# Attention and feed-forward on one core: transposes of the probabilities moved to the end of each TensorE step

## The reference

```python
q = jnp.einsum('btm,mhd->bthd', x, w_aq)
k = jnp.einsum('btm,mhd->bthd', x, w_ak)
v = jnp.einsum('btm,mhd->bthd', x, w_av)
q = _rope(q)
k = _rope(k)
s = jnp.einsum('bihd,bjhd->bhij', q, k) / D_HEAD
s = s - jnp.asarray(INF_APPROX, x.dtype) * mask
p = jax.nn.softmax(s, axis=-1)
o = jnp.einsum('bhij,bjhd->bihd', p, v)
r = jnp.einsum('bihd,hdm->bim', o, w_ao)
...
x = _layernorm(x + attention(x))
h = jax.nn.silu(_tlin(x, w1_w, w1_s)) * _tlin(x, w2_w, w2_s)
h = jax.nn.gelu(_tlin(h, h1_w, h1_s), approximate=False)
h = jax.nn.gelu(_tlin(h, h2_w, h2_s), approximate=False)
x = _layernorm(x + _tlin(h, w3_w, w3_s))
```

## Time and profile before

| | |
|---|---|
| median of 3 runs | 1065.4 us (1064.43 to 1065.68) |
| profiled execution, its own time | 1065.99 us |
| span of the profiled execution | 1064.2 us |
| PE busy | 997.1 us (94%) |
| DVE busy | 820.6 us (77%) |
| ACT busy | 593.3 us (56%) |
| POOL busy | 539.6 us (51%) |
| mean granted TensorE clock | 0.981 |

### The profile page before, as it was taken

How to read it: one execution, slowest core, us unless ns; L and a number is a source line. 1 busy time by engine, 2 the same in 40 slices (tenths; PEclk the granted TensorE clock), 3 DMA queues, 4 the chain that set the end, 5 groups by cost and what they waited for, 6 DMA issues and landing times. The chain is left out here.

```text
span 1064.2 us, 19686 instructions
## 1 busy us (share of the span) xinstructions
PE 997.1 (94%) x5648; PEld 860.2 (81%) x5648; DVE 820.6 (77%) x1803; ACT 593.3 (56%) x1255; POOL 539.6 (51%) x536
## 2 busy tenths in 40 slices
PE   3799999999999999999999999999839999999995
PEld 3688888898888889888888888888728878788784
DVE  5888888888888888887888888788555677486744
ACT  3566666665666666566666666666434252433521
POOL 4666767776676776677677666767250101000000
PEclk9899999999999999999999999999969999999998
DMA  8433233432322123323222222221020000000000
GB/s 282 150 127 74 61 80 97 124 99 56 75 69 69 49 59 100 70 61 79 59 49 59 61 70 68 72 59 40 1 80 1 1 1 21 1 20 0 1 20 21
DMA packets 33292, 66.16 MB, mean 62 GB/s; under 512 B 5457, under 2 KB 6993, under 8 KB 32209
## 3 DMA queue, kind: packets, MB, share of 16 engines
q1 hardware_dynamic: 30400, 58.62, 21.0%
q10 hardware_dynamic: 2832, 6.82, 1.7%
HBM read 24.26 MB, written 7.34 MB: 30 GB/s over the span
## 5 line engine op out<-in xcount | busy, mean ns | idle before, releaser
L703 POOL TENSOR_SCALAR probs<-probs,inv_sum 128x128 f32<-128x128 f32 (+7 forms) x256 | 191.1, 747 | 232.4 <-DVE inv_sum L621 231.8
L534 ACT ACTIVATE pT<-psum 128x512 fp32r<-128x512 f32 (+3 forms) x384 | 173.9, 490 | 144.0 <-PE psum L401 141.9
L308 PE MATMUL psum<-pT,vals 128*128 128x512 f32 (+3 forms) x1152 | 242.6, 351 | 1.6 <-DVE rT L663 1.6
L522 ACT ACTIVATE probs<-psum,neg_max 128x128 f32<-128x128 f32 (+7 forms) x256 | 190.5, 744 | 80.2 <-DVE neg_max L615 79.8
L615 DVE TENSOR_REDUCE neg_max<-psum 128x1 f32<-128x128 f32 (+7 forms) x256 | 191.2, 747 | 54.8 <-PE psum L392 53.6
L631 DVE TENSOR_TENSOR pT<-psum,pT 128x512 fp32r<-128x512 f32 (+3 forms) x384 | 200.7, 551 | 32.3 <-ACT pT L534 25.3
L308 PEld LDWEIGHTS psum<-pT,vals 128*128 128x128 f32 x1152 | 187.7, 189 | 23.9 <-DVE pT L631 1.7
L401 PE MATMUL psum<-ident,probs 128*128 128x128 f32 x1152 | 173.7, 277 | 12.9 <-POOL probs L703 12.2
L883 PE MATMUL ps<-hid,w 128*128 128x512 f32 x768 | 181.3, 396 | 0.0
L708 POOL TENSOR_TENSOR swapped<-by_cos,swapped 128x512 f32<-128x512 f32 x128 | 164.7, 1298 | 14.2 <-DMA swapped<-by_sin 14.2
L883 PEld LDWEIGHTS ps<-hid,w 128*128 128x128 f32 x768 | 143.7, 188 | 34.5
(11 more groups left out here) (77 smaller groups left out, 1195.3 us busy)
## 6 DMA issues: line engine op xcount, KB each, us to landing
swapped<-by_sin SPq DMA_DIRECT2D x256, 128.0 KB, 2.3
w_stage<-qk_split SPq DMA_DIRECT2D x30, 256.0 KB, 2.7
wv_stage<-v_split SPq DMA_DIRECT2D x15, 256.0 KB, 2.7
x_split<-ffn_raw ACTq DMA_DIRECT2D x2, 1024.0 KB, 5.8
ffn_raw<-g SPq DMA_DIRECT2D x2, 1024.0 KB, 8.0
x_moving<-x_split SPq DMA_DIRECT2D x2, 1024.0 KB, 5.1
out<-y SPq DMA_DIRECT2D x4, 512.0 KB, 2.6
raw_x<-xT SPq DMA_DIRECT2D x3, 512.0 KB, 11.6
```

The costliest lines, as they stand in the source:

```text
L308: ins = nc.tensor.matmul(out_ap, left[a], right[b], start=first and i == 0, stop=last and i == 2)
L522: nc.scalar.activation(probs[:, ib % 4, :width].rearrange("p (h c) -> p h c", h=halves), score_ps[:, ib % 2, :halves, :half], ACT.Exp, bia ...
L534: nc.scalar.activation(pT[chunk][:, 0, 4 * f:4 * f + n_blocks, (ib % 4) * P:(ib % 4 + 1) * P], bank("t", head[1], nth)[:, :n_blocks * P].r ...
L703: nc.gpsimd.tensor_scalar(p, p, inv_sum[:, n:n + 1], 1.0, ALU.mult, ALU.mult).then_inc(probs_ready[0], 1)
```

## The change

Within a step, PE now does the `qk` projections, the values and the pieces of the weighted sum right after the scores, and the transposes last. ACT takes the high part of the values ahead of that of the transposed probabilities, and DVE the rotation's products and the low part of the values ahead of the low part of the transposed probabilities. `plan_banks` follows the new order. POOL and SP are as they were.

```diff
@@ -77,9 +77,9 @@
-            after = ([("t", off, FIRST_FILL[s] + k) for k in range(FILLS_OF[s])]
-                     + [("qk", off + 1, j) for j in range(NQK) if QK_STEP[j] == s]
-                     + [("v", 0, c) for c in range(NV) if V_STEP[c] == NI * off + s])
+            after = ([("qk", off + 1, j) for j in range(NQK) if QK_STEP[j] == s]
+                     + [("v", 0, c) for c in range(NV) if V_STEP[c] == NI * off + s]
+                     + [("t", off, FIRST_FILL[s] + k) for k in range(FILLS_OF[s])])
@@ -463,8 +463,6 @@
                 if exists(ahead):
                     scores(ahead, (s + 2) % NI)
-                if exists(head):
-                    transpose_probs(head, s)
                 for target, j in rope_tasks(head, s, QK_STEP):
                     project_qk(step_on(target, -1), j)
                 for c in v_tasks(head, s):
@@ -473,6 +471,8 @@
                 if s in PV1_PIECES and exists(step_on(head, -1)):
                     attend(step_on(head, -1), 1, PV1_PIECES[s])
+                if exists(head):
+                    transpose_probs(head, s)
@@ -575,10 +575,10 @@
+                for c in v_tasks(head, s):
+                    values_high(head[0], c)
                 if exists(head):
                     transposed_high(head, s)
-                for c in v_tasks(head, s):
-                    values_high(head[0], c)
@@ -680,12 +680,12 @@
-                if exists(head):
-                    transposed_low(head, s)
                 for target, j in rope_tasks(head, s, QK_STEP):
                     rope_products(target, j)
                 for c in v_tasks(head, s):
                     values_low(head[0], c)
+                if exists(head):
+                    transposed_low(head, s)
```

## The result

The changed kernel took 1081.39 us (median of 4 runs, 1080.66 to 1082.54) against 1065.32 us before: a ratio of 1.0153, 95% interval 1.0136 to 1.0171. That is 16.1 us more; the profiled executions differ by 1080.66 - 1065.99 = 14.7 us. The forecast was 1086.5 us, with a range from 1073 to 1096.

What follows compares the result with a forecast made beforehand. PE was taken as the bound; 15 odd heads at +1.31 us (19.7), 15 even heads at +0.13 (2.0) and -0.7 at the end gave +21 us on 1065.99. Forecast 1086.5 us, range 1073 to 1096.

Steps and rivals of the forecast that it cites:

- What bounds, and what can be gained: PE bounds; odd heads' step 6 has stalls of 0.81 and 0.16 us, 0.97 us per odd head to gain.
- T to the scores of block 4, 5.62 us: Odd head, from its start (T, scores of block 2): bank 1 waits for DVE's low part of block 0, +0.72 us.
- Scores of block 4 to X, 7.62 us: Odd head, to the end of block 3's transposes (X): step 3's twelve matmuls come in ahead, +1.94 us on 5.68.
- X to the scores of block 0, 5.68 us: Block 3's transposes' end to next head's block 0 scores: POOL's low part of tile 1 sets it, -0.38 us.
- Odd head, +1.31 us: Each odd head's four stretches together: 0.72 + 1.94 - 0.38 - 0.97 us, paid by 15 odd heads.
- Even head, +0.13 us: Each of 15 even heads: 0.11 us of waiting for POOL's chain plus near misses in banks, 2.0 us in all.
- The attention's end, -0.7 us: Last head: of the 1.62 us wait for the addition into `rT`, 0.7 taken as gained; bounds 0 and 1.62.
- The sum: Whole kernel: 19.7 us from odd heads, 2.0 from even ones, -0.7 at the end, together +21 us.
- Only the POOL chain binds: Rival: DVE catches up in step 0, bank 1 costs nothing new, odd head pays 0.59 us; about 1076; chance 0.17.
- the clock swing in the attention: Rival: after each step 6 wait about 3 us run at 1.2 GHz, +45 us, about 1131; chance 0.03.
- more waits: Rival: waits for `rT` in step 1 and block 4's low part, 0.25 us in 30 heads; about 1094; chance 0.14.

Runs made afterwards that it cites:

- e9: The change with step 3 back in the old order and odd heads' banks remapped so block 0's transposes take bank 5, not 1: 1047.8 us.
- e10: The change in full, with the same bank map as e9: 1066.9 us.
- e1: The change with step 3 alone put back, its transposes ahead of the weighted sum's twelve matmuls: 1061.1 us.
- e4: The change with POOL's step 4 reordered, tile 1's low part ahead of block 5's multiplication and tile 2's rotation sum: 1068.1 us.
- e2: The change with step 7 alone put back, its transposes ahead of the weighted sum's six matmuls: 1079.5 us.
- e3: The change with steps 3 and 7 both put back in the order of before: 1061.8 us.
- e6: The kernel before, with bank 1 not lent in step 0 and nothing else: 1070.2 us.
- e5: The change with bank 1 not lent in step 0: 1084.6 us.
- e8: The kernel before with the new order in steps 6 and 7 only, and bank 1 not lent in step 0: 1083.1 us.
- e7: The change with step 3 in the order of before and bank 1 not lent in step 0: 1065.0 us.
- e11: The kernel before with the new order in steps 6 and 7 only, planner as it is (bank 1 lent in step 0): 1077.3 us.
- e12: The change with PE's order untouched, plus e10's bank map and e4's POOL order: 1054.3 us.

## Why the prediction was right, and where its terms were off

- **What bounds, and what can be gained.** Right. The stalls of step 6 in odd heads are gone, and from the scores of block 0 to the next head takes 452.79 - 448.30 = 4.49 us (forecast 4.56).
- **T to the scores of block 4, 5.62 us.** Measured 435.15 - 429.53 = 5.62 us. e9 and e10 show it as the meeting of DVE's lateness and one bank, worth 1.0 us in each odd head.
- **Scores of block 4 to X, 7.62 us.** Measured 442.70 - 435.15 = 7.55.
- **X to the scores of block 0, 5.68 us.** Measured 448.30 - 442.70 = 5.60, by the median 5.68. e1 and e4 break this chain at its two ends, TensorE's order and POOL's, and end 20.3 and 13.3 us under the change.
- **Odd head, +1.31 us.** By the medians +1.05 us. The four stretches changed by +0.72, +1.86, -0.41 and -1.13 us, where +0.72, +1.94, -0.38 and -0.97 were forecast: the waits are as forecast, and most of the difference is that groups of matmuls behind other neighbours cost a little less (below). That is 15 x 0.26 = 3.9 us less than forecast.
- **Even head, +0.13 us.** Wrong in sign: -0.19 us by the medians, a gain of 15 x 0.19 = 2.9 us where a loss of 2.0 us was forecast. X to the scores of block 0 came to 423.64 - 418.00 = 5.64 us, close to the forecast 5.68; what I had left out is the same effect of the neighbours. The stretch to X grew by 1.77 and not 1.94 us, since the twelve matmuls take 1.86 us behind the scores where they took 1.96 behind transposes, and the last stretch shrank by 0.15.
- **The attention's end, -0.7 us.** Wrong in sign: from the last head's T to the feed-forward part's first instruction it takes 788.59 - 758.60 = 29.99 us, 27.31 before: +2.7 us, outside the bounds that I had given. I had taken the wait for the addition into `rT` as partly gone. From the start of the last eight transposes to the group that waits for the addition it takes 3.35 us in the change and 3.36 before: the last piece of the weighted sum, 0.7 us, had stood in this stretch, now stands ahead of it and covers nothing, and the wait grew from 1.62 to 2.26 us. Two new waits at the last head's start (0.43 us for DVE's `pT`, 0.46 for `rT`) take the place of one of 0.45 us. These make 1.1 us; the other 1.6 us are TensorE's clock, below.
- **The sum** by these measured terms: 15 x 1.05 - 15 x 0.19 + 2.7, and 1.1 us less at the start (the first odd head's T is at 53.44, before at 54.51), is 14.5 us, against 14.7 between the profiled executions. The start may be chance: the other kernels have this T at 53.70 to 54.56.
- **The rivals.** "Only the POOL chain binds" did not happen, nor did the clock swing in the attention: 15 waits of about 1.0 us left it at full rate. Of "more waits", the bank that block 5's transposes need from block 4 is late in the change too, but this wait lies under the one for POOL and costs nothing; it shows when that one is lifted (e4).

The mechanism was right in both its parts. The forecast of 21 us against the profiles' 14.7 comes from the two terms wrong in sign and from the odd head's 0.26 us: 3.9 + 4.9 us too much, 3.4 us too little at the end, and 1.1 us not foreseen at the start; between the medians the change cost 16.1 us. That the total came within 5.1 us is in part luck, since the terms wrong in sign miss in opposite directions.

## What to carry to other kernels

Before work is moved inside a pipelined step, list what starts at the moved instruction on the other engines, and follow each in-order queue to the instruction that the bound engine waits for: here four transposes of step 3 held back, by way of ACT and DVE, the POOL instruction that PE needs in step 6. A wait for a buffer has two causes, a late reader and the choice of the buffer; a rotation that hands buffers out in turn moves the wait to another place when one use is added, so look at the whole map before and after. A moved instruction can gain and lose at once, and the losing step can be left out: the best version here (e9, 1047.8 us) is the change without its step 3 and with block 0's transposes of the odd head in another bank, for which seven other uses of banks moved too. It may not be the end: in e9's odd heads the scores of block 0 still start 0.05 to 0.13 us behind POOL's low part, after six transposes that take 1.04 us. e9 with e4's order on POOL was not run.

## What the runs showed of the hardware that I had not expected

**The clock at the end of the attention.** The last 24 matmuls of the weighted sum took 6.43 us in the change and 4.86 us before. PE's timeline and windows of the changed kernel (length, busy time of PE, PEld, DVE, ACT, POOL, granted clock, DMA):

```profile
777.75 1.09 PE L401 MATMUL psum<-ident,probs 128*128 128x128 f32 x8 [1.03 <-POOL probs L703]
...
781.10 6.43 PE L308 MATMUL psum<-pT,vals 128*128 128x512 f32 x24 [2.26 <-DVE rT L663]
```

```profile
779.00:781.00 2.00, 0.00 (x0) 0.00 (x0) 1.89 (x3) 0.53 (x2) 0.00 (x0) 1.00 0.00 0
781.00:783.00 2.00, 1.90 (x5) 1.60 (x6) 0.00 (x0) 0.00 (x0) 0.00 (x0) 0.60 0.00 0
783.00:785.00 2.00, 2.00 (x6) 1.54 (x6) 0.00 (x0) 0.00 (x0) 0.00 (x0) 0.55 0.00 0
785.00:787.60 2.60, 2.54 (x15) 2.15 (x14) 0.02 (x1) 0.00 (x0) 0.00 (x0) 1.00 0.00 0
```

After idle stretches of 1.03 and 2.26 us with eight transposes between them, TensorE ran near its lower level of 1.2 GHz for about 4 us, and then at 2.4 GHz again. In the kernel before, the wait was 1.62 us and the same 24 matmuls ran at 1.00. All fourteen kernels fall in two groups. Where step 7 has the old order (before, e2, e3, e6) a weighted-sum piece stands between the eight transposes and a wait of 1.62 or 1.63 us, and the group took 4.84 to 4.86 us. Where it has the new one, only the eight transposes stand between waits of about 1.03 and 2.26 us, and the group took 6.43 to 6.45 us in six kernels (the change, e1, e4, e5, e8, e10) and 7.46 to 7.61 us in four (e7, e9, e11, e12). The length of the wait and what stands ahead of it changed together, so which of the two lowers the clock is not shown, nor why four kernels lost 1 us more. The Trainium skill (TensorE: Matmul & The Clock Gate, section A second HAM failure mode: psum-queue depth-cycling) has frequent small idle times between groups make the clock swing between its levels; the waits of about 0.7 and 1.0 us in the attention, one of each in every pair of heads (47 us), did not.

**A group's price depends on its neighbour.** Six 512-wide matmuls of a projection take 1.47 us from start to start right behind transposes (before) and 1.38 us behind scores (change); the scores of block 5 take 1.17 us behind a weighted sum and 1.25 us behind transposes. In a step with both the two nearly cancel, which is why moving the transposes was almost free by itself. What in the array makes the difference was not tried.
